# Zeroing the attention diagonal in the probabilities on GpSimd instead of adding a mask product on TensorE

## Time and profile before

| | |
|---|---|
| runs | 1362.61, 1373.47, 1376.96 us; median 1373.47 |
| profiled execution | span 1371.2 us; no time is listed for it beside its span |
| PE busy | 1171.5 us, 85% |
| DVE busy | 698.9 us, 51% |
| ACT busy | 432.5 us, 32% |
| POOL busy | 52.9 us, 4% |
| mean granted TensorE clock | 0.881 of full speed |

### The profile page before, as it was taken

One profiled execution on the slowest core, in us unless ns is written; L12 is line 12 of the kernel. 1 busy time (PEld: TensorE's weight loads), 2 busy tenths in 40 slices (PEclk: granted clock), 3 DMA queues, 4 the chain that ended last, 5 costly groups with the idle time before them and its releaser, 6 DMA issues.

```text
span 1371.2 us, 19879 instructions
## 1 busy us (share of the span) xinstructions
PE 1171.5 (85%) x7172; PEld 790.7 (58%) x7172; DVE 698.9 (51%) x1981; ACT 432.5 (32%) x933; POOL 52.9 (4%) x89
## 2 busy tenths in 40 slices
PE   7798546586789998999899989998999999885996
PEld 4343324353457666757666766575667756662775
DVE  3467742544275357535743574466456652724242
ACT  1222103132324342434242425332533343241321
POOL 6101100000000000000000000000000000000000
PEclk9999656566789998999898999998999999996998
DMA  9200040232031204210421043004301520012000
GB/s 277 88 1 0 7 78 1 47 76 40 8 78 40 41 7 88 54 33 1 88 58 29 1 94 66 15 15 87 65 10 25 101 41 2 9 39 40 1 8 8
DMA packets 37991, 60.55 MB, mean 44 GB/s; under 512 B 4976, under 2 KB 30176, under 8 KB 37344
## 3 DMA queue, kind: packets, MB, share of 16 engines
q1 hardware_dynamic: 35504, 55.86, 19.4%
q10 hardware_dynamic: 2384, 3.30, 0.8%
HBM read 42.36 MB, written 16.34 MB: 43 GB/s over the span
## 4 chain that ended last, share of the span: by engine, by line
PE 55%; DVE 19%; issue 9%; ACT 4%; DMA 2%; SPq 1%; DVEq 0%; POOL 0%; ACTq 0%; POOLq 0%
PE PS L615 13%; PE PS L627 11%; PE PS L736 6%; PE PS L822 5%; PE PS L763 5%; PE PS L728 4%; DVE mx L1227 3%; PE PS L769 3%; PE PS L778 2%; PE PS L831 2%; ACT probs L994 1%; PE PS L837 1%; PE PS L855 1%; PE PS L867 1%; DVE rem L1108 1%
## 5 line engine op out<-in xcount | busy, mean ns | idle before, releaser
L615 PE MATMUL PS<-x2T,w 96*128 96x370 f32 x768 | 289.8, 504 | 7.2 <-issue 7.2
L627 PE MATMUL PS<-w,hid 128*128 128x192 f32 x1152 | 233.9, 342 | 7.9 <-ACT hid L640 7.6
L627 PEld LDWEIGHTS PS<-w,hid 128*128 128x128 f32 x1152 | 205.4, 201 | 47.3 <-issue 12.6
L640 ACT ACTIVATE hid<-PS,b 128x370 f32<-128x370 f32 x192 | 108.8, 568 | 383.0 <-PE PS L615 383.0
L1227 DVE TENSOR_REDUCE mx<-PS 128x2 f32<-128x356 f32 x288 | 129.8, 520 | 148.5 <-PE PS L763 105.4
L615 PEld LDWEIGHTS PS<-x2T,w 96*128 96x128 f32 x768 | 146.9, 201 | 68.5 <-issue 18.8
L994 ACT ACTIVATE probs<-PS 128x356 f32<-128x356 f32 x288 | 112.8, 485 | 29.5 <-PE PS L763 19.3
L763 PE MATMUL PS<-kst,qst 96*128 96x178 bf16 x384 | 69.5, 276 | 32.8 <-DMA kst<-scr_k 14.2
L728 PE MATMUL PS<-xT,w_at 96*96 96x370 f32 x192 | 77.1, 552 | 8.8 <-ACT q L961 5.2
L778 PE MATMUL PS<-masks,ident_bf 128*128 128x256 bf16 (+1 forms) x288 | 79.8, 278 | 0.0
L650 DVE SCALAR_TENSOR_TENSOR acc<-PS,comb,acc 128x192 f32<-128x192 f32 x96 | 34.0, 409 | 86.9 <-PE PS L627 86.9
(11 more groups left out here) (190 smaller groups left out, 1393.0 us busy)
## 6 DMA issues: line engine op xcount, KB each, us to landing
qst<-scr_q SPq DMA_DIRECT2D x96, 144.0 KB, 4.6
scr_q<-qs SPq DMA_DIRECT2D x16, 432.0 KB, 3.3
scr_k<-ks SPq DMA_DIRECT2D x16, 432.0 KB, 4.7
kst<-scr_k SPq DMA_DIRECT2D x16, 432.0 KB, 4.8
w<-in_w SPq DMA_DIRECT2D x2, 2304.0 KB, 36.8
kst<-scr_k SPq DMA_DIRECT2D x16, 288.0 KB, 5.8
cols<-in_x_cols SPq DMA_DIRECT2D x6, 392.0 KB, 14.2
kst<-scr_k SPq DMA_DIRECT2D x16, 144.0 KB, 6.3
```

The lines of the kernel that those rows point to most:

```text
L615: ins = nc.tensor.matmul(PS[:, 4 + u % 2, 0:XN], w1[:, k, 128 * u:128 * u + 128], x2T[:, k, 0:XN], start=(k == 0), stop=(k == 1))
L627: ins = nc.tensor.matmul(tile_psum((6, 7), i), hid[u % 2][:, 128 * i:128 * i + 128], w2[:, u, :], start=(j == 0 and i != 1), stop=(j == FT ...
L640: nc.scalar.activation(hid[u % 2][:, 0:XN], PS[:, 4 + u % 2, 0:XN], ACT.Relu, bias=b1[:, u:u + 1]).then_inc(S["h_ready"], 1)
```

## The change

In the exponential pass of block 0 the mask product is left out. In its place POOL runs `affine_select` on the probabilities in SBUF, behind ACT's exponential and ahead of the value products: elements whose column index equals their partition index (less 64 for the second item of bank 2) are replaced by 0, all others kept. The max pass keeps its mask product.

```diff
-        def pe_logits(pe, s, r, u, rows_, still, move, read, filled):
+        def pe_logits(pe, s, r, u, rows_, still, move, read, filled, masked):
...
-                if s == 0:
+                if masked:
...
-                pe_logits(pe, s, r, u, SROWS, qst[s], kst[s], S["s_used", s], S["s_psum", s])
+                pe_logits(pe, s, r, u, SROWS, qst[s], kst[s], S["s_used", s], S["s_psum", s], s == 0)
...
-                pe_logits(pe, s, r, u, SROWS + 3, kst[s], qst[s], S["e_done", s], S["e_psum", s])
+                pe_logits(pe, s, r, u, SROWS + 3, kst[s], qst[s], S["e_done", s], S["e_psum", s], False)
...
             pe.wait_ge(S["e_done", s], at(r, 3 * HH, 6 * g + 6))
+            if s == 0:
+                pe.wait_ge(S["p_masked"], at(r, 4 * HH, 8 * g + 8))
...
+        def pool_masks(pool, r):
+
+            for u in range(HH):
+                for bank in range(2):
+                    pool.wait_ge(S["e_done", 0], at(r, 3 * HH, 3 * u + bank + 1))
+                    plain_wait(pool)
+                    block = probs[:, u % PROB_UNITS, bank, :].rearrange("p (b j) -> p b j", b=2)[:, :, 0:NTXT]
+                    nc.gpsimd.affine_select(block, block, [[0, 2], [-1, NTXT]], ALU.not_equal, 0.0, base=0,
+                                            channel_multiplier=1).then_inc(S["p_masked"], 1)
+                pool.wait_ge(S["e_done", 0], at(r, 3 * HH, 3 * u + 3))
+                block = probs[:, u % PROB_UNITS, 2, :].rearrange("p (g j) -> p g j", g=2)[:, :, NTXT:NTXT + NI]
+                for b in range(2):
+                    plain_wait(pool)
+                    nc.gpsimd.affine_select(block, block, [[0, 2], [-1, NI]], ALU.not_equal, 0.0, base=-64 * b,
+                                            channel_multiplier=1).then_inc(S["p_masked"], 1)
+                    pool.wait_ge(S["p_masked"], at(r, 4 * HH, 4 * u + 3 + b))
...
+            if a is not None:
+                pool_masks(pool, a)
             if nxt is not None:
                 pool.wait_ge(S["res_ready", 0], at(a, 1, 1))
```

More of the change, by code:

```diff
@@ L543, in build @@
                  "qf_ready x2_ready x2T_psum x2T_ready gate_psum gate_used gl_ready ge_ready comb_ready "
-                 "h_psum h_ready h_used y_used fin_ready fin_h1 stored passed").split()
+                 "h_psum h_ready h_used y_used fin_ready fin_h1 stored passed p_masked").split()
         S.update({n: sem(n) for n in names + list(CHAIN_STEPS)})
@@ L763, in pe_logits @@
                         ins = nc.tensor.matmul(PS[:, bank, T * b:T * b + T], still[0:rows_, h, TP * b:TP * b + NTXT],
-                                               move[0:rows_, h, TP * b:TP * b + T], start=(b == 0), stop=(s == 1),
+                                               move[0:rows_, h, TP * b:TP * b + T], start=(b == 0), stop=not masked,
                                                skip_group_check=True)
@@ L771, in pe_logits @@
                                                    move[0:rows_, 2 * u + g, TP * b:TP * b + T], start=(g == 0),
-                                                   stop=(s == 1),
+                                                   stop=not masked,
                                                    skip_group_check=True)
-                if s == 0:
+                if masked:
                     own = PS[:, bank, 0:T2].rearrange("p (b j) -> p b j", b=2)
```

## The result

The changed kernel takes 1405.69 us (median of 4 runs, 1388.42 to 1406.92) against 1374.64 for the kernel before (median of 4): ratio **1.0247, 95% interval 1.0191 to 1.0303**. Measured again beside other kernels it had 1394.27 us against 1369.20: 1.0181, interval 1.0128 to 1.0234. By the medians the change costs some 25 to 31 us. The ratios leave out executions in which the chip ran in a slower state, so they need not be the quotient of the medians shown. The profiled execution of the first set took 1404.58 us with a span of 1402.9.

The account below looks back on a forecast made before the run. PE's program, taken in order, was taken to set the time. Passes at POOL's pace (+51.3 us) and the clock (+9.4) gave +60.7 on the median of 1373.5: 1434 us, range 1392 to 1480.

Parts of the forecast that it names:

- The forecast's own case: In the exponential pass of block 0, p between 2.1 and 3.5 us, giving 1410 to 1470 us; chance 0.63.
- p: POOL's time for one unit of three banks (four selects and two waits on itself), taken as 2.7 us.
- the first rival: POOL selects at the copy's rate, p = 1.84, with no fall of the clock: 1396 us; chance 0.16.
- The clock: TensorE's granted clock falls in the exponential pass, so the last value group takes 2.59 instead of 1.41 us: +9.4 us.
- The price of a select: On POOL, 0.65 and 0.45 us a select, and 0.25 us for each wait of POOL on itself.
- The term of +51.3 us: Eight exponential passes of block 0 at POOL's pace, 135.4 us, less 83.1 and less 1 us.
- 83.1: Sum in us of the kernel before's eight passes, each from first exponential to start of last value group.
- The formula for a pass: First exponential to start of last value group takes 5.9 + 4p us for p up to 2.59, else 0.6 + 6p + 0.13.
- a bound of up to 28 us: Upper bound on the clock term with p under 2.6, where value groups 0 and 1 are exposed too.
- the signs that I named: Selects under 0.4 or over 0.8 us, POOL waiting for ACT between units 2 and 3, clock at 1.00, or delay not carried.
- The removed products: 144 mask products less on PE in the exponential passes of block 0, worth at most about 6 us.
- The delay carried through: A microsecond added before a pass's last value group is added to PE's program and carried whole to the end.

Follow-up runs that it names:

- no_mask: The changed kernel without the selects and PE's wait for them, diagonal left unmasked in the exponential pass: 1361.1 us, 0.9953 of the kernel before.
- spare_selects: The changed kernel with the selects on a spare tile and PE not waiting for them, diagonal left unmasked: 1361.7 us, 0.9956 of the kernel before.
- more_selects: The changed kernel with one more select on a spare tile ahead of each text-bank select: 1429.9 us, 1.0438 of the kernel before.
- late_values: The changed kernel with value groups 0 and 1 of block 0 one unit later on PE and ACT: 1374.6 us, 1.0024 of the kernel before.
- busy_wait: The changed kernel with 7, 3 and 3 unused products ahead of PE's waits for the selects: 1382.0 us, 1.0088 of the kernel before.
- after_again: The changed kernel measured once more, unchanged, beside other kernels: 1394.3 us, 1.0181 of the kernel before.

## Why the prediction was right, and where it was off

**Direction and mechanism: right, and shown.** Slower was given 0.91, and slower it is. no_mask and spare_selects show that the removal gains and that the selects by themselves cost nothing. more_selects shows the slope of 4 on POOL's time a unit. late_values shows that it is the place of the wait that costs.

**The number: in the range by luck.** The forecast's own case was p from 2.1 to 3.5 and 1410 to 1470 us; neither held. What held is the p of the first rival, which had 0.16: POOL near the copy's rate, p between 1.5 and 2.1. Its full clock did not hold. By that rival's sum, with no fall of the clock, the measured p of 1.70 gives 8 x 12.7 - 84.1 = +17.5 us, so 1391, just under the range from 1392 on. The clock, whose cost the sum had too low, carried the time into it.

**The price of a select: the step that was mis-sized.** I took 0.65 and 0.45 us, nearer to the arithmetic rows. Measured are 0.409 and 0.281, and two in a row without a wait start 0.36 apart; (409 - 281) / 158 is 0.81 ns an element, the slope of the copies. POOL's wait on itself is 0.16 to 0.17 us plus a little issue, not 0.25. So p is 1.70, below even my low end of 1.84, instead of 2.7. The term of +51.3 us came to +13.4, against the same 83.1 and with the same 1 us. By the GPSIMD Engine Reference of the Trainium skill (section 4.1), one-input work is roughly line-rate: the trace agrees for the select, whose slope is the copy's, and I was wrong to weigh it down by the row of 96 elements.

**The formula for a pass: right to 0.6 us.** 5.9 + 4p gives 12.7 at p = 1.7; measured at full clock is 12.06. I had counted the pause behind a unit's last select, which delays the next unit but not the value group: 3.83 us to group 0 against 4.1 by the sum, then 4.12 and 4.11 against 4.3.

**The clock: right in kind, too small.** I had it fall late in the pass, for the last group only, +9.4 us. Measured: in the steady passes of the first set it falls ahead of group 0 (2.60 us in all five); in three it rises and falls again for the last group, in two it stays down through group 1: +15.5 us in the passes against the 94.4 of before. In the five steady passes alone, like for like, it is 10.9 us where my term has 5.9. I had said that groups 0 and 1 are covered while POOL works. By my own sum that is so for p over 2.6; at 1.7 POOL itself waits 2.08 us for ACT behind a slow group, so the slow group is exposed. That is the case of p under 2.6, for which I had set a bound of up to 28 us. Two of the signs that I named for the step being wrong so came true: a select under 0.4 us, and POOL waiting for ACT between units 2 and 3. The page "TensorE: Matmul & The Clock Gate" of the Trainium skill (part 1) tells the fall as what follows idleness; read as no fall for waits as short as these, of which the longest is 2.01 us, it would have missed the 10.9 us above; here the measurement decides.

**What the removed products do to the clock: left out.** I took the removed products as a gain only, and the fall of the clock as brought by the wait. By the count above it falls ahead of group 0 in 13 of 30 passes with no mask products and hardly a wait, and in none of 10 with the products and no wait; busy_wait shows that work in the wait gives part of the loss back.

**The removed products: right in time.** I had bounded them at about 6 us; 8 were measured, with an interval from 2 to 11 us.

**The delay carried through: right.** Of 26.1 us that the first seven passes grew, 24.1 are found at the start of the last one.

**So the two errors were of opposite sign:** 38 us too much for the wait, 6 too little for the clock (both against the baseline of the prediction), 2.7 of the late pass on top, and the time came out 28 us under the forecast. That it lies between the first rival's 1396 and the forecast's 1410 is no confirmation of either.

**Open:** what decides whether the clock falls in a pass, and what share of the clock's cost lies behind the passes. The profiles disagree by as much as that share, as the last section tells. Taking POOL's waits on itself away was not tried, since a race would stand in their place.

## What to carry to other kernels

Work moved to an idle engine is priced by its latency where its result is waited for, not by its busy time: 62 us on an idle POOL cost 25 to 31 us, the same work with nobody waiting cost none, and moving the consumer one unit later gave nearly all of it back (1.0024 against 1.0181). Before moving work, compare its time a unit with the pace of the engine that feeds it (1.70 against 1.11 us here), and look for the last consumer, which no order hides. Taking cheap products off TensorE can cost its clock (it fell early in 13 of 30 passes without them and without a wait, in 0 of 10 with them), so read the granted clock of the stretch together with the wait.

## What was not expected of the hardware

One stage takes two quite different lengths with the same code. Between the first two passes of block 0 lie 86 to 88 us in six of fourteen profiles, 74 to 77 in six others and 80 and 82 in the last two, and the changed kernel itself has 86.6 in its first set and 74.9 in after_again. The windows of that stage in the kernel before and in after_again (same code up to there but for the selects):

```profile
270.00:285.00 15.00, 12.64 (x27) 6.29 (x25) 3.69 (x10) 2.09 (x5) 0.00 (x0) 0.50 0.66 120
```

```profile
270.00:285.00 15.00, 11.02 (x51) 7.45 (x49) 8.90 (x19) 3.58 (x11) 0.00 (x0) 1.00 0.88 162
```

PE does 27 matmuls at a clock of 0.50 in the one and 51 at 1.00 in the other, where the clock had risen some 23 us earlier (at 267.0 against 290.3). What makes it rise early or late isn't shown. This one rise moves a span by 12 us, which is much of the scatter of the runs (1358 to 1388 us for the kernel before). It is most of why after_again's span of 1382.1 is only 10.9 over that of before while its sum is 27 over. A single span can't rank changes of under 1% here. The sums over the passes leave that stage out, but they don't rank kernels alone either: from the start of the pass of pair 2 to that of pair 7 late_values takes 659.0 us and the kernel before 664.7, though its five passes between are 6 us longer.
